# Three of sixteen input products by GpSimd, the residual sum by an identity matmul, and dtu read by VectorE from SBUF

## What is computed

```python
def mamba_block(x, Wi, cw, cb, Wx, Wdt, bdt, Alog, Dp, Wo):
    xs, z = jnp.split(x @ Wi.T, 2, axis=-1)
    u = silu(conv(xs, cw) + cb)                       # 4 taps, 256 channels
    dt, Bc, Cc = jnp.split(u @ Wx.T, [DT_RANK, DT_RANK + D_STATE], axis=-1)
    dt = softplus(dt @ Wdt.T + bdt)
    A = -jnp.exp(Alog)
    def step(h, inp):
        dt_t, B_t, C_t, u_t = inp
        dA = jnp.exp(dt_t[:, :, None] * A)
        h = dA * h + dt_t[:, :, None] * B_t[:, None, :] * u_t[:, :, None]
        return (h, jnp.einsum('bds,bs->bd', h, C_t))
    ys = scan(step, h0, ...)
    return ((ys + u * Dp) * silu(z)) @ Wo.T
for i in range(NUM_LAYERS):
    x = mamba_block(layer_norm(x), ...) + x
```

## Time and profile before

| | |
|---|---|
| median of 3 runs | 2933.65 us (2931.76 to 2934.94) |
| the profiled execution | 2935.85 us, of which the span 2934.1 us |
| DVE busy | 2104.9 us (72% of the span) |
| PE busy | 2515.8 us (86%) |
| POOL busy | 1780.1 us (61%) |
| ACT busy | 1456.5 us (50%) |
| mean granted clock of PE | 0.946 of full speed |

### The profile page before, as it was taken

The page is one execution under the profiler, slowest core; times in us unless marked ns, Lnnn a source line. Parts: engine busy times, 40 slices in busy tenths (PEclk is TensorE's granted clock), DMA queues, the critical chain, the costliest instruction groups (busy, mean ns, idle before and its releaser), DMA issues. The chain is left out here.

```text
span 2934.1 us, 27727 instructions
## 1 busy us (share of the span) xinstructions
PE 2515.8 (86%) x6470; PEld 1112.9 (38%) x6470; DVE 2104.9 (72%) x2075; ACT 1456.5 (50%) x2337; POOL 1780.1 (61%) x1090
## 2 busy tenths in 40 slices
PE   5588888888888888888888888869999999999586
PEld 3233333333333333333333333324444444444264
DVE  4399999999999999999999999972333333333221
ACT  2366657666666665666566667632222222222222
POOL 3278887888888788888888887861022202221266
PEclk9798999999999999989999999999999999999798
DMA  7334533543453344345434533516000000000154
GB/s 204 139 128 179 201 127 144 194 170 127 170 197 139 136 185 186 127 157 196 154 128 174 205 127 142 195 61 220 8 15 8 15 7 11 25 8 1 45 111 70
DMA packets 130514, 354.33 MB, mean 121 GB/s; under 512 B 21716, under 2 KB 85410, under 8 KB 97570
## 3 DMA queue, kind: packets, MB, share of 16 engines
q1 hardware_dynamic: 116770, 342.46, 32.1%
q0 software_dynamic: 11264, 7.98, 1.8%
q10 hardware_dynamic: 2432, 3.38, 0.3%
HBM read 330.34 MB, written 23.99 MB: 121 GB/s over the span
## 5 line engine op out<-in xcount | busy, mean ns | idle before, releaser
L683 POOL TENSOR_TENSOR gg<-hh,Ct 128x1024 f32<-128x1024 f32 x512 | 1205.0, 2356 | 336.2 <-DVE hh L598 322.4
L598 DVE TENSOR_TENSOR_SCAN hh<-dA,psdB 128x1024 f32<-128x1024 f32 x512 | 1170.7, 2287 | 59.4 <-ACT dA L543 6.1
L385 PE MATMUL psY<-gg,ident 128*128 128x512 f32 x2048 | 1024.4, 636 | 128.0 <-POOL gg L683 127.7
L543 ACT ACTIVATE dA<-dt,Acur 128x508 f32<-128x508 f32 x1024 | 664.6, 707 | 14.9 <-DVE hh L598 14.4
L385 PEld LDWEIGHTS psY<-gg,ident 128*128 128x128 f32 x2048 | 390.9, 200 | 689.8 <-issue 420.6
L592 DVE TENSOR_TENSOR psdB<-psU,Bt 128x1024 f32<-128x1024 f32 x512 | 617.6, 1206 | 36.8 <-ACT psU L522 36.8
L1051 DVE TENSOR_TENSOR ac<-sg,d_bank 128x512 f32<-128x512 f32 x288 | 198.1, 688 | 514.0 <-PE d_bank L901 496.8
L948 ACT ACTIVATE sg<-d_bank 128x512 f32<-128x512 f32 x288 | 171.9, 597 | 534.6 <-PE d_bank L897 521.3
L811 POOL TENSOR_TENSOR xw<-x1T,wbc 128x512 f32<-128x512 f32 x72 | 74.9, 1041 | 568.1 <-PE d_bank L901 563.8
L897 PE MATMUL d_bank<-x1T,wgu 128*128 128x512 f32 x576 | 296.6, 597 | 1.9 <-DMA wgu<-in_Wu 1.9
L901 PE MATMUL d_bank<-xw,wgu 128*128 128x512 f32 x576 | 295.5, 595 | 0.0
(11 more groups left out here) (149 smaller groups left out, 1887.1 us busy)
## 6 DMA issues: line engine op xcount, KB each, us to landing
Bt<-rows SPq DMA_DIRECT2D x128, 1024.0 KB, 6.0
Ct<-rows SPq DMA_DIRECT2D x128, 1024.0 KB, 4.7
wcur<-taps_l SPq DMA_DIRECT2D x33, 512.0 KB
disp<-zrow SPq DMA_DIRECT2D x16, 528.0 KB, 12.1
dx<-disp SPq DMA_DIRECT2D x16, 528.0 KB, 6.5
wcur<-in_W_inT SPq DMA_DIRECT2D x33, 128.0 KB
diag<-diags_l SPq DMA_DIRECT2D x33, 128.0 KB
ad_gb<-in_gb SPq DMA_DIRECT2D x32, 128.0 KB, 3.3
```

What stands on the lines that cost most here:

```text
L385: ins = pe.matmul(psY[:, :], lhsT=ident[:, :], rhs=gg[k % NGB][:, j, :], start=False, stop=(k % NK == NK - 1 and j == 1))
L543: ins = act.activation(dA[k % NDA][:, j, :, 1:T], dt[p][:, c, :, 1:T], ACT.Exp, scale=Acur[p][:, s:s + 1])
L598: dve.tensor_tensor_scan(out=hh[k % NHB][:, :, :].rearrange("p c t -> p (c t)"), data0=dA[k % NDA][:, :, :, :].rearrange("p c q t -> p (c ...
L683: pool.tensor_tensor(gg[k % NGB][:, :, :], hh[k % NHB][:, :, :], Ct[:, s:s + 2, :], ALU.mult).then_inc(prod, 1)
```

## The change

Four things are done at once, all in `mamba_phase`:

1. `dtu` stays in SBUF, in two buffers; `place_dtu`, its two PSUM tiles and its semaphore go. DVE's input product now reads both of its inputs, `dtu` and `Bt`, from SBUF.
2. Of the 16 input products of a group three (k = 4, 9 and 13, the table `GIVEN`) are made by POOL, into one of two SBUF tiles `given`, behind its `gg` of step 0, 5 and 8. ACT copies each to the PSUM buffer `dB` (`move_given`), ahead of its decay of step k + 1; DVE's scan of that step waits for the copy.
3. The residual sum leaves POOL: PE adds `h_res` to the output projection by one more matmul with the identity (128 x 512) in the same PSUM accumulation, and ACT's `added` writes the sum to `h_res` instead of `delta`. The last group's sum moves from DVE to ACT.
4. The loads of `Bt` wait for DVE's scans instead of its products.

```diff
-ACT_AT = {1: ["params", "dtu1"], ... 12: ["softplus", "sums0"], 13: ["centre"], 14: ["added"], 15: ["dtu0"]}
+ACT_AT = {1: ["params"], ... 12: ["softplus", "sums0"], 13: ["centre"], 14: ["added"]}
+GIVEN = {4: 0, 9: 5, 13: 8}
-POOL_AT = {3: ["gate1"], 6: ["rstd"], 10: ["dt"], 11: ["dtu"], 12: ["gate0"], 13: ["residual"]}
+POOL_AT = {3: ["gate1"], 6: ["rstd"], 10: ["dt"], 11: ["dtu"], 12: ["gate0"]}
...
-                    for tile, at, ld, freed in ((Bt, 0, b_ld[j], dbu), (Ct, NS, c_ld[j], prod)):
+                    for tile, at, ld, freed in ((Bt, 0, b_ld[j], scan), (Ct, NS, c_ld[j], prod)):
...
+                    pe.matmul(psW[:, :], lhsT=ident[:, :], rhs=h_res[:, ds((b - 1) % NG * G, G), :].rearrange("p q d -> p (q d)"), start=True, stop=False)
...
-                def place_dtu(t, c):
-                    act.wait_ge(dtu_ok, CR + t + 1)
-                    at_least(act, dbu, CR + NSTEP * (t - 1) + NK * (c + 1))
-                    act.activation(psU[c][:, :], dtu[:, c, :], ACT.Copy).then_inc(placed, 1)
...
                 def added(b):
                     act.wait_ge(wready, use(b, OUTP) + 1)
-                    at_least(act, res_ok, CR + b - 1)
-                    act.activation(delta[:, :], psW[:, :], ACT.Copy).then_inc(wfree, 1)
+                    act.activation(h_res[:, ds((b - 1) % NG * G, G), :].rearrange("p q d -> p (q d)"), psW[:, :], ACT.Copy).then_inc(wfree, 1)
+
+                def move_given(i, p, k):
+                    act.wait_ge(gave, CR + helped(i, k))
+                    at_least(act, scan, CR + NSTEP * i + k + 1 - NDB)
+                    act.activation(dB[k % NDB][:, :, :], given[(p + helped(0, k) - 1) % 2][:, :, :], ACT.Copy).then_inc(moved, 1)
...
                 def body(i, p, prev, more):
                     for k in range(NSTEP):
+                        if k - 1 in GIVEN:
+                            move_given(i, p, k - 1)
...
+                    if k in GIVEN:
+                        return
                     at_least(dve, scan, CR + n + 1 - NDB)
-                    dve.tensor_tensor(dB[k % NDB][:, :, :], psU[c][:, :].unsqueeze(1).broadcast_to([128, 2, TOK]), Bt[:, s:s + 2, :], ALU.mult).then_inc(dbu, 1)
+                    dve.tensor_tensor(dB[k % NDB][:, :, :], dtu[p][:, c, :].unsqueeze(1).broadcast_to([128, 2, TOK]), Bt[:, s:s + 2, :], ALU.mult).then_inc(dbu, 1)
...
+                    if k in GIVEN:
+                        dve.wait_ge(moved, CR + helped(i, k))
+                    else:
+                        dve.wait_ge(dbu, CR + made(i, k))
...
-                def residual(b):
-                    pool.wait_ge(wfree, use(b, OUTP) + 1 - isinstance(b, int))
-                    at = ds((b - 1) % NG * G, G)
-                    pool.tensor_tensor(h_res[:, at, :], h_res[:, at, :], delta[:, :].rearrange("p (q d) -> p q d", q=G), ALU.add).then_inc(res_ok, 1)
...
+                def give(i, p, k):
+                    c, s = k // NK, 2 * (k % NK)
+                    if c == 0:
+                        pool.wait_ge(b_ld[s // CKS], 16 * (i + 1))
+                    at_least(pool, moved, CR + helped(i, k) - 2)
+                    pool.tensor_tensor(given[(p + helped(0, k) - 1) % 2][:, :, :], dtu[p][:, c, :].unsqueeze(1).broadcast_to([128, 2, TOK]), Bt[:, s:s + 2, :], ALU.mult).then_inc(gave, 1)
```

More of the change, by code:

```diff
@@ L276, in mamba_phase @@
         dt = [sb(f"dt{p}", [128, NH, G, T]) for p in range(2)]
-        delta = sb("delta", [128, TOK])
         soft = sb("soft", [128, NH, TOK])
-        dtu = sb("dtu", [128, NH, TOK])
+        dtu = [sb(f"dtu{p}", [128, NH, TOK]) for p in range(2)]
+        given = [sb(f"given{b}", [128, 2, TOK]) for b in range(2)]
         xd = sb("xd", [64, TOK])
@@ L287, in mamba_phase @@
         dB = [ctx.enter_context(nc.psum_tensor(f"psdB{b}", [128, 2, TOK], f32)) for b in range(NDB)]
-        psU = [ctx.enter_context(nc.psum_tensor(f"psU{c}", [128, TOK], f32)) for c in range(NH)]
         psY = ctx.enter_context(nc.psum_tensor("psY", [128, TOK], f32))
@@ L316, in use, with made, helped @@
             return CR + WUSE * b + WUSE - 1 + c
+        def made(i, k):
+            return len([a for a in range(k + 1) if a not in GIVEN]) + (NSTEP - len(GIVEN)) * i
+        def helped(i, k):
+            return len([a for a in GIVEN if a <= k]) + len(GIVEN) * i
         def at_least(eng, sm, v):
@@ L397, in out_projection @@
                             ins = pe.matmul(psW[:, q * T:(q + 1) * T], lhsT=yg[p][:, c, q * T:(q + 1) * T],
-                                            rhs=wo[:, ds((b - 1) // NG * NH + c, 1), :].rearrange("p o m -> p (o m)"), start=(c == 0), stop=(c == NH - 1))
+                                            rhs=wo[:, ds((b - 1) // NG * NH + c, 1), :].rearrange("p o m -> p (o m)"), start=False, stop=(q == G - 1 and c == NH - 1))
                     ins.then_inc(wready, 1)
@@ L453, in last @@
                     pe.wait_ge(wfree, use(NIT - 1, OUTP + 1) - 1)
+                    pe.matmul(psW[:, :], lhsT=ident[:, :], rhs=h_res[:, (NG - 1) * G:NG * G, :].rearrange("p q d -> p (q d)"), start=True, stop=False)
                     for q in range(G):
                         for c in range(NH):
-                            ins = pe.matmul(psW[:, q * T:(q + 1) * T], lhsT=yg[1][:, c, q * T:(q + 1) * T], rhs=wo[:, (NL - 1) * NH + c, :], start=(c == 0), stop=(c == NH - 1))
+                            ins = pe.matmul(psW[:, q * T:(q + 1) * T], lhsT=yg[1][:, c, q * T:(q + 1) * T], rhs=wo[:, (NL - 1) * NH + c, :], start=False, stop=(q == G - 1 and c == NH - 1))
                     ins.then_inc(wready, 1)
@@ L462, in _ @@
             def _(act):
-                for sm in (par_ok, soft_ok, exp_ok, ln_ok, da, wfree, silu_ok, centred, placed, ycopied):
+                for sm in (par_ok, soft_ok, exp_ok, ln_ok, da, wfree, silu_ok, centred, ycopied, moved):
                     act.sem_inc(sm, CR)
@@ L551, in first, with last @@
                     centre(1)
-                    place_dtu(0, 0)
+                def last():
+                    copy_sums(NIT - 1, 1, 1)
+                    act.wait_ge(wready, use(NIT - 1, OUTP + 1) + 1)
+                    act.activation(h_res[:, (NG - 1) * G:NG * G, :].rearrange("p q d -> p (q d)"), psW[:, :], ACT.Copy)
                 def body(i, p, prev, more):
                     for k in range(NSTEP):
+                        if k - 1 in GIVEN:
+                            move_given(i, p, k - 1)
                         for what in ACT_AT.get(k, ()):
@@ L560, in body @@
                                 centre(i + 2)
[L561 to L564, removed]
                             if prev and what == "added":
@@ L571, in body @@
                         decay(i, p, k)
-                loop(act, body, first, lambda: copy_sums(NIT - 1, 1, 1))
+                loop(act, body, first, last)
             @block.vector
@@ L583, in _, with input_term, scan_step @@
                 dve.wait_ge(zeroed, 1)
-                def input_term(i, k):
+                def input_term(i, p, k):
                     n, c, s = NSTEP * i + k, k // NK, 2 * (k % NK)
-                    if s == 0:
-                        dve.wait_ge(placed, CR + NH * i + c + 1)
+                    if k == 0:
+                        dve.wait_ge(dtu_ok, CR + i + 1)
                     if c == 0 and s % CKS == 0:
                         dve.wait_ge(b_ld[s // CKS], 16 * (i + 1))
+                    if k in GIVEN:
+                        return
                     at_least(dve, scan, CR + n + 1 - NDB)
-                    dve.tensor_tensor(dB[k % NDB][:, :, :], psU[c][:, :].unsqueeze(1).broadcast_to([128, 2, TOK]), Bt[:, s:s + 2, :], ALU.mult).then_inc(dbu, 1)
-                def scan_step(n, k):
+                    dve.tensor_tensor(dB[k % NDB][:, :, :], dtu[p][:, c, :].unsqueeze(1).broadcast_to([128, 2, TOK]), Bt[:, s:s + 2, :], ALU.mult).then_inc(dbu, 1)
+                def scan_step(i, k):
+                    n = NSTEP * i + k
                     dve.wait_ge(da, CR + n + 1)
-                    dve.wait_ge(dbu, CR + n + 1)
+                    if k in GIVEN:
+                        dve.wait_ge(moved, CR + helped(i, k))
+                    else:
+                        dve.wait_ge(dbu, CR + made(i, k))
                     at_least(dve, prod, CR + n + 1 - NHB)
@@ L602, in statistics @@
                     g = t % NG
-                    at_least(dve, res_ok, CR + t - 7)
+                    at_least(dve, wfree, use(t - 2, 0))
                     at_least(dve, moments, CR + t)
@@ L623, in body @@
                                 statistics(i + 2)
[L624 to L633, removed]
+                        input_term(i, p, k)
+                        scan_step(i, k)
+                loop(dve, body, first, lambda: None)
             @block.gpsimd
             def _(pool):
-                for sm in (prod, rstd_ok, dt_ok, dtu_ok, ygated, res_ok):
+                for sm in (prod, rstd_ok, dt_ok, dtu_ok, ygated, gave):
```

(13 more changed lines are left out.)

8 lines of the change are left out of this document (4 added, 4 removed).

## The result

The changed kernel takes 3209.41 us (median of 4 runs, 3205.91 to 3210.58) against 2933.16 for the kernel before (median of 4): a ratio of 1.0939, 95% interval 1.092 to 1.0958. It is 276 us slower. The forecast was 3240 us, with a range of 3050 to 3560.

What follows compares the result with a forecast made beforehand. DVE was taken to set the pace at 57.1 us a group; afterwards POOL's 52.8 plus 12.6 of turns (walk 65.5) plus 1.2 for lost turns gave 66.7, 9.6 x 32 = 307 us more: 3240 us, range 3050 to 3560.

Steps and rivals of the forecast that it cites:

- The hold-up: DVE's product with two SBUF inputs and POOL's instructions shut each other out; a product takes 0.97 us of POOL's time.
- The sum: POOL's 52.8 us a group of own work plus 12.6 for turns with 13 products: 65.4 us.
- The walk: One Mamba group followed in order, turns alternating: eight products meet a running POOL instruction, 65.5 us a group.
- Few instances at 1.2: Sign in the profile after: few of DVE's products (L592) would take their undisturbed 1.2 us; mean about 2,100 ns.
- the term for lost turns: Held products sometimes letting a further POOL instruction by, at most 2.32 us each: taken as 1.2 us a group.
- The copies "hidden, at nothing": ACT's three copies of given products, 1.06 us each, bring ACT to 39 of 57 us a group: no cost.
- the rival "faster": DVE's 53.5 and POOL's 52.8 us would bound a group, 54.5 with waiting: 2850 us; chance 0.09.
- Lost turns as a rule: Rival: DVE gets through only when POOL runs out of work, 79.4 us a group: 3645 us, half 3420; chance 0.14.
- Milder hold-up: Rival: POOL frees DVE earlier in its long instructions, 59 to 62 us a group: 2995 to 3090 us; chance 0.13.
- No hold-up: Rival: a product that writes PSUM does not meet POOL, so the price is zero: 2850 us; chance 0.09.
- The late copies: Rival: step 13's product and ACT's copy reach the scan late, +125 us: 3365; its chance lies within the forecast's 0.62.
- Loads of Bt: POOL's product for step 4 needs Bt's third chunk early, 5 us to spare; release by scans 2.3 us later: no cost.

Runs made afterwards that it cites:

- e8: e1 with one product given to POOL (step 4, made behind step 0) instead of three: 2881.1 us, ratio 0.9813 to the kernel before.
- e9: e1 without its third given product (step 13), so steps 4 and 9 remain: 2869.0 us, ratio 0.9772 to the kernel before.
- e5: The kernel before with only the residual moved to PE's identity matmul, no products given to POOL: 2932.4 us, ratio 0.999.
- e1: The changed kernel with dtu again copied to PSUM by ACT and read there by DVE's products: 2886.4 us, ratio 0.9833 to the kernel before.
- e2: The kernel before with only dtu kept in SBUF, read there by all 16 products; none given, residual on POOL: 3239.4 us, ratio 1.1033.
- e7: e1 with two products given to POOL, steps 4 and 14, instead of three: 2899.0 us, ratio 0.987 to the kernel before.

## Why the prediction was right

**The bound before and the undisturbed costs.** DVE set the pace: taking products from it (e8, e9) makes the kernel faster, taking work from POOL and giving it to PE (e5) does nothing that can be told.

**The hold-up.** It was read off three places of the trace of before, none in the Mamba phase, and it holds in the new place with the same numbers: each held product ends 1.09 us after POOL's end (forecast 1.07), each of the 319 held ggs 2.19 to 2.22 after DVE's (2.22). The rule of the Trainium skill ("SBUF — State Buffer", Who interferes with whom) agrees with the trace for these pairs. Where both engines have work in store, products and POOL's instructions alternate.

**The sum.** Forecast for POOL was 52.8 us of its own work and 12.6 of turns. In the stretch, gg is 2940 - 2357 = 0.58 us longer (16 times: 9.3), the given product some 0.32 (3: 1.0), the gate 0.50 (2: 1.0) and `negm` 0.97: 12.3. With 52.8 and the 1.0 a group that POOL still idles that is 66.1, and 66.0 is measured. DVE stands 13 x (2244 - 1207) = 13.5 us a group; the forecast was 12. The walk named eight products a group that would be held (steps 2, 5, 6, 10, 11, 12, 14, 15), and 256 / 32 = 8 are, but at steps 0, 2, 5, 7, 10, 11, 12 and 15 (in 31 or 32 groups each): six of the steps are right, and that the number is too is in part luck. "Few instances at 1.2" was wrong by the walk's own count: five of 13 are undisturbed. 65.5 us a group would have been 3202 us.

**Where it was off.** The 31 us between 3240 and 3209 come from the term for lost turns, 1.2 us a group or 38 us; without it the forecast would have been 7 us low. The term was taken from one instance of L235 in the setup phase. None of the 416 products lost a turn. But L235 is no accident either: its first instance waits for the last of the taps in the trace of every kernel here, 1.30 to 2.07 us long, and in e1 (where it is L236) it was issued into the second of four and let two more go by.

```profile
L236 DVE SCALAR_TENSOR_TENSOR ad_nrm<-ad_y,ad_mv,ad_gb x32: 337/352/2069, 26.2 to 79.2; 128x128 f32<-128x128 f32 x32
```

Its next instances run beside POOL's `diags` (a TENSOR_SCALAR with one SBUF tensor) in 0.45 us and end before it does, so not every POOL instruction shuts DVE out to its end. L216 keeps its turn in every trace in which a tap holds it. Why L235 loses turns where L216 and the products don't isn't known. (The 0.46 us that the prediction gives as the rows' largest hold-up is L216's; L235 was held for 1.11.)

**A term at half its size.** The prediction put the residual's matmul of 128x512 at 0.63 us, the mean of L385. The trace has two records for each such matmul (892 for 14 groups of 32), and in the changed kernel the residual's has two records of 614 ns. PE has the room, so nothing came of it.

**The right number, from a sum that doesn't carry over.** POOL's work plus the turns (65.4) and the walk in order (65.5) agreed in the prediction, and I took e2's expectation from the sum alone: 62.7, measured 67.0. The sum holds only while POOL always has a scan in store. With fewer instructions on POOL, DVE's own list sets the pace, with each wait in it. That the forecast came so near owes something to this case being one where POOL hardly idles.

**The copies "hidden, at nothing".** In the changed kernel that is so: the scans' idle time is 8 us in 800, none of it for a copy. Without the hold-up (e1) the scans wait 3.1 us a group for ACT, and the figure of the rival "faster", 2850, was 36 us too low for that. The prediction had looked at ACT's sum (39 of 57 us) and at the time from scan k-2 to scan k, and not at what stands in front of the copy in ACT's list; in e7 that holds the copy up.

**The rivals.** Lost turns as a rule: excluded by the maximum of 3387. Milder hold-up: excluded by the handover, 1.09 us at each of the 256 held products. No hold-up: excluded by e1 against the change, at 323 us. The late copies: not in the changed kernel. Loads of Bt: in the Mamba phase POOL waits for no DMA.

**From SBUF or PSUM.** The product's shortest time is 1204 ns from SBUF; in the kernel before it was 1203 from PSUM. The Trainium skill's difference in the fixed part ("VectorE: DVE Perf Modes", the TRN2 errata), an estimate of 0.065 us, doesn't show.

## What to carry to other kernels

Before one moves an operand of a VectorE instruction from PSUM to SBUF, count its SBUF inputs: with two, the product here took turns with GpSimd's elementwise instructions on SBUF, and a copy to PSUM that looks like waste (here 1.2 us a group on ScalarE, which had room) can be what keeps the two apart (323 us). A part of a change that costs nothing should be asked what covers it, and for an engine that runs a list in order the answer is what stands in front of it, not the engine's sum. Of the change, e9 keeps what helps: two products given, at steps 4 and 9, the residual by PE, dtu in PSUM: 2869 us, 2.3% below before.

## What was not expected of the hardware

- A POOL instruction of 128x4 elements is held up too: `negm`, a TENSOR_SCALAR with one input from SBUF, takes 1197 ns at the median beside 228 before.

```profile
L655 POOL TENSOR_SCALAR negm<-mv x33: 224/1197/1297, 82.5 to 2143.6; 128x4 f32<-128x4 f32 x33
```

- The held instruction is booked as busy, not as idle: in e2 POOL and DVE show 724 and 779 us busy of 800, and the kernel is 10% slower than the one with 659 and 776.
- PE idled more before its matmuls of L393 (270.8 us over the span, 128.0 for the same line before) and was granted a mean of 0.915 of its full clock over the span instead of 0.946, and its matmul of 128x512 (L393) takes 684 ns instead of 636. It isn't on the path here: it waits for POOL.
